# Attention in a two-layer graph network: scores of two steps together, outputs summed in the transposes' banks, other matmuls dealt out 12, 18, 12, 6

## The reference

```
# layer 0
x = layernorm(x + (adj @ x @ weight + bias))
# layer 1, per batch entry
q, k, v = split(x @ w_qkv)                       # 8 heads of 64
attn = softmax(where(adj == 0, -inf, (q @ k.T) * scale))
o = (attn @ v) @ w_proj + b_proj
ln = (o - mean(o)) * rsqrt(var(o) + 1e-5) * gamma + beta
x = layernorm(x + o + ln)
```

## Time and profile before

| | |
|---|---|
| median of 3 runs | 3786.73 us (3784.12 to 3786.85) |
| profiled execution, span from first to last instruction | 3783.6 us |
| mean granted TensorE clock | 0.991 |
| PE busy | 3694.9 us, 98% |
| PEld busy | 2865.1 us, 76% |
| DVE busy | 2911.8 us, 77% |
| ACT busy | 2164.6 us, 57% |
| POOL busy | 1533.9 us, 41% |

### The profile page before, as it was taken

One profiled execution on the slowest core, in us unless ns is written; L12 is line 12 of the kernel. 1 busy time (PEld: TensorE's weight loads), 2 busy tenths in 40 slices (PEclk: granted clock), 3 DMA queues, 4 the chain that ended last, 5 costly groups with the idle time before them and its releaser, 6 DMA issues.

```text
span 3783.6 us, 64102 instructions
## 1 busy us (share of the span) xinstructions
PE 3694.9 (98%) x18960; PEld 2865.1 (76%) x18960; DVE 2911.8 (77%) x6681; ACT 2164.6 (57%) x4505; POOL 1533.9 (41%) x2311
## 2 busy tenths in 40 slices
PE   8999999989999999999999999999999999999996
PEld 6888888867777777777777777777777777777775
DVE  7666666636888888888888888888888787888887
ACT  4444444436666666666666666666666666666664
POOL 4555555522333333333333333333333333333334
PEclk9999999989999999999999999999999999999998
DMA  6555555530111111111111111111111111111111
GB/s 195 177 177 177 177 177 177 177 105 27 45 44 44 44 44 44 44 44 47 47 44 44 45 49 44 44 44 50 44 44 44 50 44 44 44 44 44 44 52 35
DMA packets 344957, 276.18 MB, mean 73 GB/s; under 512 B 13664, under 2 KB 275808, under 8 KB 344928
## 3 DMA queue, kind: packets, MB, share of 16 engines
q1 hardware_dynamic: 344928, 275.83, 24.1%
HBM read 141.56 MB, written 134.22 MB: 73 GB/s over the span
## 4 chain that ended last, share of the span: by engine, by line
PE 71%; DVE 4%; ACT 2%; issue 1%; POOL 0%; DVEq 0%; POOLq 0%
PE bank L764 20%; PE bank L778 10%; PE bank L730 10%; PE bank L796 10%; PE bank L719 9%; PE bank L745 7%; PE bank L746 6%; DVE pt_lo L931 3%; ACT pt_hi L838 1%; ACT v L849 1%; DVE probs L917 0%; DVE o_stats L957 0%; POOL probs L663 0%; DVE ot L949 0%; DVE v L942 0%
## 5 line engine op out<-in xcount | busy, mean ns | idle before, releaser
L830 ACT ACTIVATE probs<-probs,bias_row 128x512 f32<-128x512 f32 x1024 | 731.5, 716 | 441.2 <-DVE bias_row L917 441.2
L931 DVE TENSOR_TENSOR pt_lo<-bank,pt_hi 128x512 fp32r<-128x512 f32 x1024 | 694.4, 689 | 287.5 <-ACT pt_hi L838 264.7
L838 ACT ACTIVATE pt_hi<-bank 128x512 fp32r<-128x512 f32 x1024 | 556.9, 596 | 513.7 <-PE bank L730 513.7
L663 POOL TENSOR_SCALAR probs<-probs,inv_sums 128x480 f32<-128x480 f32 (+1 forms) x1024 | 687.1, 684 | 0.0
L917 DVE CUSTOM_DVE_ANT_0 probs<-bank,mask_bias 128x512 f32<-128x512 f32 x1024 | 661.5, 683 | 1.2 <-PE bank L719 1.2
L660 POOL TENSOR_TENSOR probs<-probs,inv_sums 128x32 f32<-128x32 f32 x512 | 123.3, 241 | 1155.9 <-DVE inv_sums L923 1155.6
L730 PE MATMUL bank<-ident,probs 128*128 128x128 f32 x4096 | 535.9, 274 | 15.6 <-POOL probs L663 13.7
L730 PEld LDWEIGHTS bank<-ident,probs 128*128 128x128 f32 x4096 | 480.8, 141 | 89.0 <-POOL probs L663 19.3
L669 POOL TENSOR_TENSOR o_rstd<-o_var_eps,half_neg 128x1 f32<-128x1 f32 x256 | 156.9, 613 | 725.7 <-DVE o_var_eps L962 725.7
L745 PE MATMUL bank<-pt_hi,v 128*128 128x512 f32 x1024 | 413.8, 404 | 26.6 <-DVE pt_lo L931 22.0
L764 PE MATMUL bank<-x_hi,w_hi 128*128 128x512 f32 x1024 | 411.8, 402 | 11.4 <-PEq L209 11.4
(11 more groups left out here) (90 smaller groups left out, 7654.0 us busy)
## 6 DMA issues: line engine op xcount, KB each, us to landing
x_in<-in_x_dram SPq DMA_DIRECT2D x32, 1024.0 KB, 5.6
ut_hi<-ut_hi_sb SPq DMA_DIRECT2D x128, 256.0 KB, 3.7
ut_lo<-ut_lo_sb SPq DMA_DIRECT2D x128, 256.0 KB, 3.7
u_beta_rows<-ub SPq DMA_DIRECT2D x32, 1024.0 KB, 4.4
x_hi<-ut_hi SPq DMA_DIRECT2D x128, 256.0 KB, 4.2
x_lo<-ut_lo SPq DMA_DIRECT2D x128, 256.0 KB, 4.6
out_dram<-o SPq DMA_DIRECT2D x128, 256.0 KB, 3.1
ub_row<-u_beta_rows SPq DMA_DIRECT2D x124, 256.0 KB, 2.9
```

The costliest lines, as they stand in the source:

```text
L663: pool.tensor_scalar(probs[:, k % 2, a, cols], probs[:, k % 2, a, cols], inv_sums[:, k % 4, a:a + 1], 0.0, ALU.mult, ALU.add)\
L830: act.activation(probs[:, k % 2, a, :], probs[:, k % 2, a, :], ACT.Exp, bias=bias_row[:, k % 4, a:a + 1], scale=-1.0, accum_out=sums[:, k ...
L838: act.activation(pt_hi[:, a, :, n * P:(n + 1) * P], t_bank[a][:].rearrange("p (m n) -> p m n", m=T), ACT.Copy)\
L931: dve.tensor_tensor(pt_lo[:, a, :, cols], t_bank[a][:].rearrange("p (m n) -> p m n", m=T), f32(pt_hi[:, a, :, cols]), ALU.subtract).then_i ...
```

## The change

There are four edits, all in the second stage, and all on the order of the work and on the banks. What is computed stays the same, and so does the number of instructions.

1. `scores` of steps k + 2 and k + 3 are issued together, ahead of `turn(k)`, at every even k. They have four banks (0 to 3), two for each step.
2. `attend_v` writes into the banks of the transposes (now 4 and 5): `o_bank = t_bank`. The four banks of the scores need the room. So `turn` at the start of a group waits for `ot_summed` in place of `ptlo_made`, and `ot_halves` (ACT) and `ot_sum` (DVE) stand at the end of a group's fourth step, where before they stood in the first two steps of the next group.
3. The filling matmuls, 48 in each group, are dealt out as 12, 18, 12 and 6 over the four steps in place of 16, 16, 16 and 0. In the fourth step they come before `attend_v`, which takes keys 0 to 2 of both heads first and then key 3 of both.
4. On DVE, ACT and POOL the small parts move: `inverse` and `normalise` are those of step k + 2 at the end of step k (before: k + 1 at the start of step k), `LN_STEP` is one step earlier, and each bank of the filling matmuls is evacuated at the step after it is complete, or for the fourth in the same step.

```
-            s_bank, t_bank, o_bank, g_bank = psum[0:2], psum[2:4], psum[4:6], psum[6:8]
+            s_bank, t_bank, g_bank = (psum[0:2], psum[2:4]), psum[4:6], psum[6:8]
+            o_bank = t_bank
...
-            LN_STEP = [7, 9, 11, 13]
+            LN_STEP = [6, 8, 10, 12]
+
+            FILL = [12, 18, 12, 6]
+            BEFORE = [sum(FILL[:n]) for n in range(T)]
...
-            def output_at(b, k, j):
-                if j == 2 and k == 6:
-                    return None
-                if k % T == j or (j == 2 and k == 7):
+            def output_at(b, k):
+                if k == T - 1 + T:
+                    return (b, 0)
+                if k % T == 1 and k != 1 + T:
                     return (b - 1, PAIRS - 1) if k < T else (b, k // T - 1)
...
# POOL, batch
-                            if k + 1 < STEPS or more:
-                                normalise(b, k + 1)
                             if last_part and row_at(k - 1, LN_STEP) is not None:
                                 add_ub(b, row_at(k - 1, LN_STEP))
                             if last_part and row_at(k, O_STEP) is not None:
                                 power(b, row_at(k, O_STEP), 0)
+                            if k + 2 < STEPS or more:
+                                normalise(b, k + 2)
...
# PE, scores: the wait for the bank's last reader, and the bank
-                                pe.wait_ge(max_found, b * 32 + (2 * k + a - 1))
+                                pe.wait_ge(max_found, b * 32 + (2 * k + a - 3))
...
# PE, turn
-                            if not (isinstance(b, int) and b * STEPS + k == 0):
+                            if k % T:
                                 pe.wait_ge(ptlo_made, b * 32 + (2 * k + a - 1))
+                            elif not (isinstance(b, int) and b * STEPS + k == 0):
+                                pe.wait_ge(ot_summed, b * 8 + (k // 2 + a - 1))
...
# PE, attend_v
-                        for a in range(2):
-                            pe.wait_ge(ptlo_made, b * 32 + (8 * p + 7 + a))
-                            if a == 0:
+                        for keys in ((0, 1, 2), (3,)):
+                            for a in range(2):
+                                if 0 in keys:
+                                    pe.wait_ge(ptlo_made, b * 32 + (8 * p + 7 + a))
                                 if p == 0:
-                                    pe.wait_ge(vlo_made, b * 4 + 4)
+                                    pe.wait_ge(vlo_made, b * 4 + keys[-1] + 1)
...
# PE, batch
-                            turn(b, k)
-                            if k + 2 < STEPS or more:
-                                scores(b, k + 2)
                             group, part = divmod(k, T)
+                            if k % 2 == 0 and (k + 2 < STEPS or more):
+                                scores(b, k + 2)
+                                scores(b, k + 3)
+                            turn(b, k)
+                            if group == 0:
+                                v_matmuls(b, BEFORE[part], FILL[part])
+                            elif group == 1 and last_part:
+                                project(b, BEFORE[part], FILL[part])
+                            elif group >= 2 and more:
+                                qk_matmuls(b + 1, 48 * (group - 2) + BEFORE[part], FILL[part])
                             if part == T - 1:
                                 attend_v(b, group)
...
# ACT, batch
-                            if k == 3:
-                                unit_hi(b, k, 3, more)
                             pt_hi_part(b, k)
-                            if k % T == 3 and k > 3:
-                                unit_hi(b, k, 3, more)
                             if last_part and row_at(k - 2, LN_STEP) is not None:
                                 result(b, row_at(k - 2, LN_STEP))
...
                             if k + 2 < STEPS or more:
                                 exponent(b, k + 2)
-                            if k % T < 3:
-                                unit_hi(b, k, k % T, more)
+                            unit_hi(b, k, k % T, more)
+                            if output_at(b, k) and (last_part or k >= T):
+                                ot_hi_part(*output_at(b, k))
+                            if k % T == T - 1:
+                                ot_halves(b, k // T)
...
# DVE, batch
-                            if k + 1 < STEPS or more:
-                                inverse(b, k + 1)
-                            if k % T in (1, 2):
+                            if k % T:
                                 unit_lo(b, k, k % T - 1, more)
...
+                            if k % T == T - 1:
+                                unit_lo(b, k, T - 1, more)
+                            if ahead:
+                                inverse(b, k + 2)
+                            if output_at(b, k) and (last_part or k >= T):
+                                ot_lo_part(*output_at(b, k))
+                            if k % T == T - 1:
+                                ot_sum(b, k // T)
```

More of the change, by code:

```diff
@@ L690, in batch @@
                                 power(b, row_at(k, O_STEP), 0)
+                            if k + 2 < STEPS or more:
+                                normalise(b, k + 2)
                     normalise(0, 0)
+                    normalise(0, 1)
                     batch(0, last_part=False)
@@ L713, in scores @@
                         for a in range(2):
-                            if not (isinstance(b, int) and b * STEPS + k == 0):
-                                pe.wait_ge(max_found, b * 32 + (2 * k + a - 1))
+                            if not (isinstance(b, int) and b * STEPS + k < 2):
+                                pe.wait_ge(max_found, b * 32 + (2 * k + a - 3))
                         for i, (l, r) in enumerate(parts):
@@ L718, in scores @@
                                 h = slice(a * HEAD, (a + 1) * HEAD)
-                                last = pe.matmul(s_bank[a][:], l[h, pair, n * P:(n + 1) * P], r[h, pair, :],
+                                last = pe.matmul(s_bank[k % 2][a][:], l[h, pair, n * P:(n + 1) * P], r[h, pair, :],
                                                  start=i == 0, stop=i == 2)
@@ L734, in attend_v @@
                     def attend_v(b, p):
-                        for a in range(2):
-                            pe.wait_ge(ptlo_made, b * 32 + (8 * p + 7 + a))
-                            if a == 0:
+                        for keys in ((0, 1, 2), (3,)):
+                            for a in range(2):
+                                if 0 in keys:
+                                    pe.wait_ge(ptlo_made, b * 32 + (8 * p + 7 + a))
                                 if p == 0:
-                                    pe.wait_ge(vlo_made, b * 4 + 4)
-                                if not (isinstance(b, int) and b * PAIRS + p == 0):
-                                    pe.wait_ge(ot_summed, b * 8 + 2 * p)
-                            for m in range(T):
-                                w = v[:, m, 2 * p + a, :, :].rearrange("p s d -> p (s d)")
-                                pe.matmul(o_bank[a][:], w, pt_hi[:, a, m, :], start=m == 0, stop=False)
-                                last = pe.matmul(o_bank[a][:], w, pt_lo[:, a, m, :], start=False, stop=m == T - 1)
-                            last.then_inc(pv_done, 1)
+                                    pe.wait_ge(vlo_made, b * 4 + keys[-1] + 1)
+                                for m in keys:
+                                    w = v[:, m, 2 * p + a, :, :].rearrange("p s d -> p (s d)")
+                                    pe.matmul(o_bank[a][:], w, pt_hi[:, a, m, :], start=m == 0, stop=False)
+                                    last = pe.matmul(o_bank[a][:], w, pt_lo[:, a, m, :], start=False,
+                                                     stop=m == T - 1)
+                                if 3 in keys:
+                                    last.then_inc(pv_done, 1)
                     def qk_matmuls(b, first, count, begin=False):
@@ L1006, in batch @@
                             ahead = k + 2 < STEPS or more
-                            if k + 1 < STEPS or more:
-                                inverse(b, k + 1)
-                            if k % T in (1, 2):
+                            if k % T:
                                 unit_lo(b, k, k % T - 1, more)
-                            elif k == 3:
-                                unit_lo(b, k, 3, more)
-                            if last_part and k == O_STEP[3]:
-                                add_bproj(b, 3)
                             pt_lo_part(b, k, ahead)
@@ L1019, in batch @@
                                 masked_max(b, k + 2, waited=True)
-                            for j, stage_of in ((1, ot_sum), (2, ot_lo_part)):
-                                if output_at(b, k, j) and (last_part or k >= T):
-                                    stage_of(*output_at(b, k, j))
```

(12 more changed lines are left out.)

17 lines of the change are left out of this document (3 added, 14 removed).

## The result

The changed kernel takes 3905.97 us (median, 3904.14 to 3907.17) against 3786.79 (3784.12 to 3787.06) for the kernel before on the same chip: 1.0319 times as long [1.0306, 1.0331], 119 us slower. The forecast was 3910. The profiled execution took 3905.5 us, its span is 3903.6, 120.0 longer than before, and its mean granted clock 0.988. PE is now busy for 93% of the span.

What follows compares the result with a forecast made beforehand. PE's own pace was taken as the bound. Per entry 88.1 us of PE work plus 7.7 of waits made 95.8 against 91.86; over 31 entries 122 us, so 3783.6 + 122 + 3.1, given as 3910 us, range 3800 to 3985.

Steps and rivals of the forecast that it cites:

- PE alone: PE's time per batch entry without waits: 91.5 less 3.4 us from joining the scores, so 88.1.
- The block of scores: On PE, two steps' scores issued together take 1.80 us, of which 0.42 is extra cost at the block's ends.
- Sum of the waits: PE's new waits in one batch entry: 1.0 + 1.3 + 3.2 + 1.1 + 1.1 = 7.7 us.
- Fourth step: PE's wait before `attend_v` in a group's fourth step: 1.0 us, taken as 1.1 each in groups 2 and 3.
- here lies the cost: Third and fourth steps 3.67 us apart, so `attend_v` waits for `pt_lo`: chain 6.9 us, PE ready at 5.9.
- with nothing queued: Argument that the 6.9 us chain from the third step's transposes to `attend_v` comes from trace rows without queued work.
- ACT's order: ACT works in order, so the next step's `pt_hi` starts only after `unit_hi` ends, at about 5.4 us.
- Key 3: In group 0, `attend_v` on key 3 waits 1.3 us for the fourth bank of V.
- Group 1: DVE runs late: `attend_v` waits 2.2 us, the next transposes 0.7 and 0.3 for the sums; together 3.2.
- `ot_lo` 24.0, sums 24.7: End of DVE's schedule in group 1, us from group start: `ot_lo` done at 24.0, first output sum at 24.7.
- The outputs' sums in every group: Rival: output sums come late in all groups, 2 us more in groups 0, 2 and 3; 4094 us, chance 0.07.
- The clock: Rival: group 1's waits lower PE's clock once an entry, 3.5 us each, 108 us in all; 4018 us, chance 0.07.

Runs made afterwards that it cites:

- e2: Changed kernel with scores issued one step at a time, still ahead of the transposes, four score banks and shared output banks kept: 3959.90 us.
- e1: Changed kernel with the filling matmuls dealt out 12, 12, 16, 8 in place of 12, 18, 12, 6: 3872.13 us.
- e10: Changed kernel with eight of step 8's twelve filling matmuls put ahead of its transposes, into PE's wait for the output sums: 3906.15 us.
- e4: Changed kernel with the third Q/K bank evacuated a step later in groups 2 and 3, behind `pt_hi` and `pt_lo`: 3899.96 us.
- e7: Changed kernel with V's fourth bank, in step 3, copied on ACT before the exponential and subtracted on DVE before `masked_max`: 3901.63 us.
- e6: Changed kernel with the normalised rows a step later, `LN_STEP` back at 7, 9, 11, 13: 3875.74 us.
- e3: Changed kernel with step 7 reordered: on DVE `ot_lo` before the projection row, sums and `inverse` before the statistics; POOL normalises first: 3869.98 us.
- e5: Changed kernel with the earlier banks (outputs their own pair) and scores one step at a time behind the transposes; deal and new order kept: 3803.21 us.
- e8: Changed kernel with the edits of e3, e4 and e7 together: 3799.26 us, 1.0038 times the kernel before.
- e9: Changed kernel with the edits of e3, e4, e7 and e6 together: 3826.83 us, 1.0110 times the kernel before.
- e11: e7 plus eight extra matmuls, no part of the result, in PE's wait ahead of step 8's transposes: 3868.59 us.

## Why the prediction was right, and where it was not

- *PE alone.* Forecast 88.1 an entry; it is 87.6. A step of 12 matmuls takes 3.72 from transposes to transposes (forecast 3.67), and one of 18 with the joined scores 6.75 (6.87), together 10.47 for 10.54. The block of scores was mis-sized: 10.47 - 2 x 0.87 - 2.80 - 4.20 = 1.73, not 1.80, so its ends cost 0.35 in the changed kernel; e2 has 0.36. The forecast read 0.42 from the earlier trace rows.
- *Sum of the waits.* Forecast 7.7 an entry, measured 7.7. This is in part luck, since the terms were off both ways.
- *Fourth step.* Forecast 1.0 in group 0 and 1.1 in groups 2 and 3; measured 0.7, 0.85 and 0.86. Place and releaser were right. The reason, "here lies the cost" of steps 3.67 apart, was wrong in groups 2 and 3. The step that fails there is "with nothing queued": the forecast started the chain at the third step's transposes and looked at the last two steps alone. But in the second step of a group DVE also makes `ot_lo` of the group before, which waits for ACT's `ot_hi` behind the exponentials and a copy, and then `k_lo`. DVE's rows in group 3:

```profile
1666.35 0.69 DVE L957 TENSOR_TENSOR ot_lo<-ot,ot_hi 128x512 fp32r<-128x512 f32 x1 [0.83 <-ACT ot_hi L876]
1666.95 0.68 DVE L941 TENSOR_TENSOR k_lo<-bank,k_hi 128x512 fp32r<-128x512 f32 x1
1667.56 1.28 DVE L935 TENSOR_TENSOR pt_lo<-bank,pt_hi 128x512 fp32r<-128x512 f32 x2
```

So `pt_lo` of the third step starts without idle time behind them, whenever its transposes came. Starts in us from the start of the group:

| | transposes of the third step | `pt_lo` of the four steps | `attend_v` |
|---|---|---|---|
| changed kernel, group 2 | 10.83 | 1.32, 6.40, 12.15, 16.94 | 17.69 |
| e1, group 2 | 9.85 | 1.33, 6.40, 12.09, 16.88 | 17.61 |
| e10, group 2 | 9.81 | 1.29, 6.36, 12.05, 16.83 | 17.57 |
| changed kernel, group 3 | 10.46 | 1.32, 6.12, 11.80, 16.59 | 17.33 |
| e1, group 3 | 9.57 | 1.32, 6.12, 11.81, 16.60 | 17.33 |

The chain runs through ACT and DVE from the group's first transposes to `attend_v`, over all four steps. PE's work moved by up to 1.0 us within it, and the chain did not. It is e4, which takes a copy out of it, that starts `attend_v` earlier (16.9 in group 3). In groups 0 and 1 DVE does idle before the third `pt_lo` (0.13 and 1.53), and there e1 gains.
- *ACT's order.* `pt_hi` of odd steps starts right behind the evacuation, as forecast:

```profile
1647.67 0.71 ACT L840 ACTIVATE probs<-probs,bias_row 128x512 f32<-128x512 f32 x1
1648.38 0.57 ACT L854 ACTIVATE q_hi<-bank 128x512 fp32r<-128x512 f32 x1
1648.86 1.06 ACT L848 ACTIVATE pt_hi<-bank 128x512 fp32r<-128x512 f32 x2
```

- *Key 3.* Forecast 1.3, measured 1.0; e7 shows it to be V's place on ACT and DVE.
- *Group 1.* Before `attend_v` forecast 2.2, measured 1.9, and e6 shows its cause. At the sums forecast 0.7 + 0.3, measured 2.0 and 0.36. Here a term was mis-sized: the step "`ot_lo` 24.0, sums 24.7" took ACT's copies as done by then. They wait for `ot_lo` themselves, so copy and sum come one after the other behind it; and POOL added the 0.52 that the forecast had named in its bounds. e3 confirms the link.
- *The outputs' sums in every group.* They are hidden in three groups of four, as the forecast read it; the rival in which each group pays would have given 4094.
- *The clock.* As a rival it was worth 108 us, once an entry at 3.5. In the changed kernel it made 4 entries longer by 1.3 each, 5 of the 120 us. A drop of the clock was one of the forecast's own signs of being wrong; it came, and was small. But the forecast's reason against it (that blocks of 1.4 us and more around a wait would keep the clock up) does not hold: in e7 it made 23 longer. Nothing in the forecast told 4 from 23, so this part is luck.
- *What is open.* How the 103 us of e5 divide between the shared banks, the joining and the place of the scores ahead of the transposes. e2 undid the joining alone, with the scores still ahead of the transposes, and its entry came out longer. Why a small edit elsewhere (e4, e7) changes in how many entries the clock falls was not found.

## What to carry to other kernels

When you take work off the engine that bounds a kernel, work out at once how long the chains of the other engines are that run beside it, over a whole period and not between two steps: here 3.9 us saved an entry met 7.7 us of waits. A wait that such a chain causes moves when its place is filled (e10). Reordering the chain itself gave time back here (e3, e4, e7, e8), as long as the work that was moved did not come to stand ahead of the next link (e9). Judge a small edit by stretches with the same granted clock, since e7 took 1.1 us off an entry, some 34 us, and lost nearly all of it to the clock.

## What the runs showed of the hardware

- After an idle time of 1.7 to 2.0 us on PE (2.6 in e2), the granted clock fell in some entries and not in others of identical code, for some eight matmuls (0.43 apart in place of 0.23). With eight matmuls in the wait it never fell behind that wait (e10, e11: none of 30 entries each, against 23 in e7 and 4 in the changed kernel).
- Where the clock falls ahead of a wait it costs nothing. In e4 the window of step 7 (11.55 us, as long as it was) has a mean clock of 0.85. Where the wait behind it has been filled or taken away, the same fall costs 1.3 (e10) or 1.0 (e3).
- A block of matmuls on 64 rows costs 0.35 us more than its matmuls, both ends together (0.36 in e2; 0.42 as read from the earlier trace rows).
